# A six-layer windowed-attention stack on one core: the mask goes to VectorE, key norms move into the score banks, and all five instruction orders are rewritten

## The reference

```python
def attn_layer(x, Wqkv, qs, ksc, Wo):                 # 16 heads of 64, windows of 32 tokens
    q, k, v = split(x @ Wqkv)
    q = rotate(l2norm(q) * qs, scale)                 # q*cos + rotate_half(q)*sin
    k = rotate(l2norm(k) * ksc, 1 / scale)
    sim = einsum(q, [previous window of k, own window of k]) * 8.0
    sim = where(mask, -big, sim)                      # a query sees its own 32 keys before it and itself
    return (softmax(sim) @ v) @ Wo
def ffn_layer(x, g, bln, W1, b1, W2, b2):             # 128 -> 2 x 341 -> 128
    xn = (x - mean) / sqrt(var + 1e-5) * g + bln
    a, gate = split(xn @ W1 + b1)
    return a * gelu(gate) @ W2 + b2
for i in range(6):
    x = attn_layer(shift_tokens(x), ...) + x          # half of the features come from the token before
    x = ffn_layer(shift_tokens(x), ...) + x
```

## Time and profile before

| | |
|---|---|
| three runs | 2286.56, 2294.89, 2439.66 us; median 2294.89 us |
| profiled execution | 2313.61 us, span of the instructions 2311.9 us |
| busy, share of the span | PE 89%, DVE 70%, POOL 40%, ACT 39% |
| mean granted TensorE clock | 0.931 of 2.4 GHz |

### The profile page before, as it was taken

How to read it: one execution, slowest core, us unless ns; L and a number is a source line. 1 busy time by engine, 2 the same in 40 slices (tenths; PEclk the granted TensorE clock), 3 DMA queues, 4 the chain that set the end, 5 groups by cost and what they waited for, 6 DMA issues and landing times.

```text
span 2311.9 us, 48227 instructions
## 1 busy us (share of the span) xinstructions
PE 2061.6 (89%) x20232; PEld 920.0 (40%) x20232; DVE 1622.5 (70%) x2739; ACT 911.6 (39%) x1388; POOL 922.6 (40%) x726
## 2 busy tenths in 40 slices
PE   5999948999999999899999999999999998999984
...
DMA packets 104046, 131.55 MB, mean 57 GB/s; under 512 B 28530, under 2 KB 48144, under 8 KB 103824
## 3 DMA queue, kind: packets, MB, share of 16 engines
...
## 4 chain that ended last, share of the span: by engine, by line
PE 52%; DVE 24%; POOL 9%; SPq 5%; ACT 4%; DMA 3%; issue 3%; POOLq 0%; DVEq 0%; ACTq 0%
PE ps_z L1065 11%; PE ps_r L983 8%; SPq L427 4%; DVE t L724 4%; PE ps_s L1041 4%; PE ps_z L1016 4%; PE ps_z L991 4%; POOL prob L500 3%; POOL prob L496 3%; DMA t<-t 3%; PE ps_z L1058 3%; DVE sinv L756 2%; DVE prob L752 2%; DVE t L657 2%; PE ps_r L1093 2%
## 5 line engine op out<-in xcount | busy, mean ns | idle before, releaser
L724 DVE TENSOR_TENSOR t<-ps_r,rot 128x1024 f32<-128x1024 f32 x384 | 461.5, 1211 | 209.6 <-PE ps_r L983 151.2
L983 PE MATMUL ps_r<-xs,w_qk_sb 128*128 128x512 f32 x768 | 430.4, 643 | 96.8 <-ACT sq L552 96.7
L552 ACT ACTIVATE sq<-ps_r 128x512 f32<-128x512 f32 x384 | 229.0, 596 | 499.9 <-DVE t L724 497.1
L490 POOL TENSOR_TENSOR q_hat<-t 128x512 f32<-128x512 f32 x192 | 243.6, 1270 | 322.0 <-DMA t<-t 322.0
L1065 PE MATMUL ps_z<-z,vo 128*128 128x512 f32 x768 | 350.0, 599 | 2.2 <-ACT z L574 2.2
L490 POOL TENSOR_TENSOR k_hat<-t 128x512 f32<-128x512 f32 x192 | 243.6, 1273 | 266.0 <-DMA t<-t 265.8
L496 POOL TENSOR_TENSOR prob<-prob,rnorm 128x1024 f32<-128x1024 f32 x96 | 182.7, 1903 | 375.5 <-DVE prob L752 375.5
L574 ACT ACTIVATE z<-ps_z 128x512 f32<-128x512 f32 x384 | 213.4, 601 | 201.2 <-PE ps_z L1058 200.0
L983 PEld LDWEIGHTS ps_r<-xs,w_qk_sb 128*128 128x128 f32 x768 | 122.5, 192 | 318.4 <-ACT sq L552 217.8
L1041 PEld LDWEIGHTS ps_s<-k_hat,q_hat 64*32 64x32 f32 x12288 | 199.7, 115 | 91.1 <-issue 91.1
L1041 PE MATMUL ps_s<-k_hat,q_hat 64*32 64x64 f32 x12288 | 232.6, 230 | 0.0
...
## 6 DMA issues: line engine op xcount, KB each, us to landing
t<-t SPq DMA_DIRECT2D x1536, 64.0 KB, 2.0
...
z<-q_hat SPq DMA_DIRECT2D x128, 16.0 KB
...
```

Of the source, the lines that this page charges most:

```text
L490: nc.gpsimd.tensor_tensor(dst, t12[:, slot, 0, :], t2[:, slot, :], ALU.add).then_inc(added.sem, 1)
L552: nc.scalar.activation(sq[:, n % SQ_SLOTS, :], ps_r[n % 2][:, :], ACT.Square).then_inc(squared.sem, 1)
L724: nc.vector.tensor_tensor(t12[:, slot, :, :], ps_r[n % 2][:, :].unsqueeze(1).to_broadcast([P, 2, SEQ]), rot[:, n // PAIRS, :, :], ALU.mult ...
L983: nc.tensor.matmul(ps_r[n % 2][:, :], w_qk_sb[:, n, :], xs[:, seq, WIN:WIN + SEQ], start=True, stop=True).then_inc(projected.sem, 1)
```

## The change

1. **Mask.** A score step now fills both banks of a tile, without the mask product: 64 small products, ordered so that even heads (rows 0 to 63, bank 0) and odd heads (rows 64 to 127, bank 1) take turns after every four. There are four score steps a unit instead of eight. DVE **mask** adds the mask while it moves both banks to `prob` (SBUF), **max** reads `prob`, and a new POOL step **lower** subtracts the maximum. `prob` has three slots instead of two. The next score step waits for the mask step of the tile before, where before it waited for the subtraction of two steps earlier.
2. **Norms.** sums 0 and 1, nturn 0, nback and the spreads use the banks `ps_s` instead of `ps_z`. The key factors are split into three bf16 parts (`split_rk`, four more small DVE instructions), so that nback and the eight spread products run in bf16.
3. **Two DMAs a chunk.** Features of a head are stored in pairs (`PAIRED`, on the host), so the swap is between neighbouring partitions: two DMAs of 64 rows with a partition step of 2 instead of four of 32 rows.
4. **Later feed-forward.** It has lag 3 instead of 1 and 2; `xg` is gone (`gain` writes `xc`), x1 waits for `new` of the unit before; `load_ffn` is issued one sequence later.
5. **Order.** All four tables are new.

```diff
 TENSOR_STEPS = [
-    ("rows", 0, 2), ("score", 0, 1), ("nturn", 1, 1), ("hid", 0, 2), ("score", 3, 1), ("hid", 1, 2), ("score", 2, 1),
+    ("out", 0, 2), ("project", 15, 1), ("nback", 0, 1), ("mean", 0, 3), ("xturn", 0, 1), ("spread", 0, 1),
...
-                for r in range(4):
-                    there = r + 1 - 2 * (r % 2)
-                    sync.dma_start(t2[WIN * there:WIN * (there + 1), slot, :],
-                                   t12[WIN * r:WIN * (r + 1), slot, 1, :]).then_inc(swapped[slot].sem, 16)
+                for odd in range(2):
+                    sync.dma_start(t2[1 - odd::2, slot, :], t12[odd::2, slot, 1, :]).then_inc(swapped[slot].sem, 16)
...
+                elif kind == "lower":
+                    pool.wait_ge(top_found.sem, top_found.at(u, n))
+                    s = prob[:, (TT * u + n) % P_SLOTS, :, :, :].rearrange("p c e n -> p (c e) n")
+                    nc.gpsimd.tensor_tensor(s, s, top[:, (TT * u + n) % P_SLOTS, :].unsqueeze(2).to_broadcast([P, HEADS, 2 * WIN]), ALU.subtract).then_inc(lower.sem, 1)
                 elif kind == "scale":
                     pool.wait_ge(normed.sem, normed.at(u, 1))
-                    pool.wait_ge(lowered.sem, lowered.all(u, (2 * n, 2 * n + 1)))
+                    pool.wait_ge(lower.sem, lower.at(u, n))
...
+            def split_rk(u):
+                dve.wait_ge(n_settled.sem, n_settled.done(u))
+                nc.vector.tensor_copy(hi, whole).then_inc(n_split.sem, 1)
+                dve.wait_ge(n_split.sem, n_split.done(u, 0))
+                nc.vector.tensor_tensor(rest, whole, hi, ALU.subtract).then_inc(n_split.sem, 1)
+                dve.wait_ge(n_split.sem, n_split.done(u, 1))
+                nc.vector.tensor_copy(mid, rest).then_inc(n_split.sem, 1)
+                dve.wait_ge(n_split.sem, n_split.done(u, 2))
+                nc.vector.tensor_tensor(low, rest, mid, ALU.subtract).then_inc(normed.sem, 1)
...
-                    nc.vector.tensor_tensor(k, k, ps_z[:, 2:4, :], ALU.mult).then_inc(keyed.sem, 1)
+                    nc.vector.tensor_tensor(k, k, ps_s[:, :, :], ALU.mult).then_inc(keyed.sem, 1)
+                elif kind == "mask":
+                    dve.wait_ge(scored.sem, scored.at(u, n))
+                    nc.vector.tensor_tensor(prob[:, (TT * u + n) % P_SLOTS, :, :, :].rearrange("p c e n -> p e c n"), ps_s[:, :, :].rearrange("p e (c n) -> p e c n", n=2 * WIN),
+                                            band[:, 0 if n == 0 else 1, :].unsqueeze(1).unsqueeze(1).to_broadcast([P, 2, PAIRS, 2 * WIN]), ALU.add).then_inc(masked.sem, 1)
                 elif kind == "max":
...
-                elif kind == "sub":
...
-                        ins = nc.tensor.transpose(ps_z[:, 2, P * t:P * (t + 1)], rk_pad[:, t, :], ident[:, :])
+                        ins = nc.tensor.matmul(ps_s[:, 0, P * t:P * (t + 1)], rk_pad[:, t, :], ident_bf[:, :], start=True, stop=True)
...
-                        ins = nc.tensor.matmul(ps_z[:, 2 + k, :], sel_rows[WIN * j:WIN * (j + 1), n // 2, :], rk_rows[WIN * j:WIN * (j + 1), :],
+                        ins = nc.tensor.matmul(ps_s[:, k, :], sel_rows_bf[WIN * j:WIN * (j + 1), n // 2, :], rk_rows[WIN * j:WIN * (j + 1), :],
...
-                    t, e = n // 2, n % 2
-                    pe.wait_ge(lowered.sem, lowered.at(u, n - 2) if t else lowered.at(u - 1, n - 2 + 2 * TT))
+                    pe.wait_ge(masked.sem, masked.at(u, n - 1) if n else masked.at(u - 1, TT - 1))
...
-                    nc.tensor.matmul(ps_s[:, e, :], ident_bf[:, :], band_bf[:, 0 if t == 0 else 1, :].unsqueeze(1).to_broadcast([P, PAIRS, 2 * WIN]),
-                                     start=True, stop=False, skip_group_check=True)
-                    rows = slice(64 * e, 64 * e + 64)
                     for c in range(PAIRS):
-                        for w in range(4):
...
+                        for e in range(2):
+                            rows = slice(64 * e, 64 * e + 64)
+                            for w in range(4):
```

More of the change, by code:

```diff
@@ L79 @@
-    ("project", 10, 0), ("out", 0, 1), ("nturn", 0, 0), ("project", 11, 0), ("out", 1, 1), ("project", 12, 0),
-    ("nback", 0, 0), ("project", 13, 0), ("spread", 0, 0), ("out", 2, 1), ("project", 14, 0), ("spread", 1, 0),
-    ("project", 15, 0), ("out", 3, 1), ("spread", 2, 0), ("sums", 2, 0), ("mean", 0, 1), ("spread", 3, 0),
-    ("vo", 0, 1), ("var", 0, 1), ("sums", 3, 0), ("score", 1, 0),
+    ("out", 0, 2), ("project", 15, 1), ("nback", 0, 1), ("mean", 0, 3), ("xturn", 0, 1), ("spread", 0, 1),
@@ new lines @@
+    ("sums", 3, 1), ("var", 0, 3), ("out", 1, 2), ("rows", 0, 3), ("spread", 1, 1), ("out", 2, 2), ("spread", 2, 1),
+    ("nturn", 1, 1), ("hid", 0, 3), ("spread", 3, 1), ("out", 3, 2), ("vo", 0, 2), ("hid", 1, 3), ("score", 0, 1),
+    ("hid", 2, 3), ("score", 1, 1), ("project", 0, 0), ("score", 2, 1), ("down", 0, 3), ("project", 1, 0),
+    ("xturn", 1, 1), ("project", 2, 0), ("score", 3, 1), ("project", 3, 0), ("mix", 0, 1), ("project", 4, 0),
+    ("project", 5, 0), ("mix", 1, 1), ("project", 6, 0), ("project", 7, 0), ("sums", 0, 0), ("project", 8, 0),
@@ L83 @@
+    ("project", 9, 0), ("mix", 2, 1), ("project", 10, 0), ("sums", 1, 0), ("project", 11, 0), ("nturn", 0, 0),
+    ("project", 12, 0), ("mix", 3, 1), ("project", 13, 0), ("project", 14, 0), ("sums", 2, 0),
 ]
 VECTOR_STEPS = [
-    ("max", 6, 2), ("sub", 7, 2), ("sub", 6, 2), ("rotate", 2, 1), ("flip", 2, 2), ("rotate", 3, 1), ("psum", 3, 2),
-    ("rotate", 4, 1), ("rotate", 5, 1), ("flip", 3, 2), ("rotate", 6, 1), ("rotate", 7, 1), ("rotate", 8, 1),
-    ("rotate", 9, 1), ("rotate", 10, 1), ("newton", 0, 1), ("rotate", 11, 1), ("rotate", 12, 1), ("rotate", 13, 1),
@@ L88 @@
-    ("keyed", 0, 1), ("rotate", 14, 1), ("keyed", 1, 1), ("rotate", 15, 1), ("x1", 0, 2), ("keyed", 2, 1),
-    ("center", 0, 2), ("keyed", 3, 1), ("rstd", 0, 2), ("max", 1, 1), ("gain", 0, 2), ("sub", 1, 1), ("max", 0, 1),
-    ("newton", 1, 1), ("gated", 0, 2), ("sub", 0, 1), ("max", 3, 1), ("sub", 3, 1), ("gated", 1, 2), ("max", 2, 1),
-    ("sub", 2, 1), ("psum", 0, 1), ("max", 5, 1), ("gated", 2, 2), ("max", 4, 1), ("flip", 0, 1), ("psum", 1, 1),
-    ("sub", 5, 1), ("sub", 4, 1), ("new", 0, 2), ("rotate", 0, 0), ("max", 7, 1), ("flip", 1, 1), ("rotate", 1, 0),
@@ L93 @@
-    ("psum", 2, 1),
+    ("newton", 0, 1), ("rotate", 13, 1), ("rotate", 14, 1), ("rotate", 15, 1), ("center", 0, 3), ("keyed", 0, 1),
+    ("rstd", 0, 3), ("keyed", 1, 1), ("gain", 0, 3), ("keyed", 2, 1), ("keyed", 3, 1), ("gated", 0, 3),
+    ("newton", 1, 1), ("gated", 1, 3), ("mask", 0, 1), ("max", 0, 1), ("gated", 2, 3), ("mask", 1, 1),
+    ("rotate", 0, 0), ("max", 1, 1), ("mask", 2, 1), ("max", 2, 1), ("new", 0, 3), ("psum", 0, 1), ("rotate", 1, 0),
+    ("x1", 0, 2), ("rotate", 2, 0), ("flip", 0, 1), ("psum", 1, 1), ("mask", 3, 1), ("rotate", 3, 0), ("max", 3, 1),
@@ L110 @@
+    ("pnorm", 0, 3), ("scale", 2, 3), ("add", 0, 2), ("add", 1, 2), ("pnorm", 1, 3), ("add", 2, 2), ("lower", 3, 3),
+    ("add", 3, 2), ("scale", 3, 3), ("pnorm", 2, 3), ("add", 4, 2), ("add", 5, 2), ("add", 6, 2), ("pnorm", 3, 3),
+    ("add", 7, 2),
 ]
@@ L436, in swap @@
                     load_vo(layer + 1)
[L437 removed]
+                if seq == 2 and c == 2 and layer:
                     sp.wait_ge(x_new.sem, x_new.done(layer * BATCH - 1))
```

170 lines of the change are left out of this document (84 added, 86 removed).

## The result

The changed kernel takes 2173.65 us (median of four runs, 2169.41 to 2175.08) against 2306.3 us for the kernel before (median of four; one of them, 2439.66 us, is from a slower state of the chip and is left out of the ratio). The ratio of the times is 0.945, 95% interval 0.937 to 0.953: faster by 5.5%. The forecast was 2095 us, range 2015 to 2200. The profiled execution took 2173.78 us, span 2172.1.

The account below looks back on a forecast made before the run. PE bounds the old kernel, DVE next. Stretches of 24.8, 36.3 and 6.8 us plus 0.9 layer work, 1.6 clock dip and 0.6 hand-overs give 71.0 us a unit; with the ends, span 2112, forecast 2095 us, range 2015 to 2200.

Parts of the forecast that it names:

- TensorE's work: PE's work in one unit falls from 71.9 to 62.8 us through mask product (2.4), scores (3.4) and norms (3.3).
- score tile: Score step of 128 instructions for both banks: 1.2 us, near full overlap of the row halves (1.03; without overlap 2.06).
- the rival of the dear DMA: Swap DMAs: an issue of 64 rows costs twice, a chunk takes 2.5 us again; +5 a unit, about 2210 us; chance 0.06.
- Stretch B: From the first score to the last pnorm, POOL's lowers, other passes and adds set the pace while PE waits: 36.3 us.
- C: End of a unit: last flip, PE's wait, last mix, two projections and sums: 6.8 us.
- 10 us of slack: DVE stays at 58 us a unit and keeps 10 us of slack, so masks on DVE leave the time at the forecast.
- stretch A: From the first out to the first score, PE runs without a pause: 24.8 us; DVE has its slack here.
- The ends: Part-filled passes at start and end: first center at 491 us, 86 us for the last passes, last center at 2068.
- the clock dip of 1.6 us: After a pause PE runs 3.5 us at 0.55 of full speed; one such dip a unit, as now, adds 1.6 us.
- the factor 0.992: From profiled execution to median time: the earlier profiled run was 0.8% above its median, so 2114 becomes 2097 us.
- The slower rival: Score tile: taking turns stops the overlap inside a bank, a tile takes 7.4 us, some 2670 us in all; slower: chance 0.04.
- The rival that the mask on VectorE only trades work: Mask step: moving the mask to DVE could simply trade PE work for DVE work; no separate chance given.

Follow-up runs that it names:

- the roots in PSUM: The changed kernel with the scratch of its inverse square roots kept in PSUM's score and sum banks instead of SBUF: 2116.2 us, 0.9195 of the kernel before.

## Why the prediction was right, and where it was off

**TensorE's work.** 62.8 us a unit was forecast, 63.15 came. The mask product is confirmed (0.27 for 0.30), the spreads too (0.32 for 0.3). The score tile was mis-sized, 1.41 for 1.2: of the 1.03 us that full overlap of two steps would save, 0.65 is saved, 0.40 of it by taking turns.

**SyncE and the rival of the dear DMA.** The rival is out: 64 rows cost what 32 do (596 and 590 ns by the medians). Halving the issues is worth 50 us on the old kernel alone and 93 us in the new one. The forecast priced a chunk of 2.5 us at 5 us a unit; 93 us are 3.9 a unit. The runs say that this is the largest single part, that tile overlap and mask product are worth 21 and 26, and that the parts don't add up: each frees a stretch that another engine then paces.

**Stretch B, "the chain is on POOL".** This step failed. Its length was nearly right (from the first score to the next out, B and C, 44.16 us, 1326.03 to 1370.19, for 43.1), but for the wrong engine. GpSimd really runs nearly without gaps in the second part, and that was read as the pace. Without 7.6 us of GpSimd's work nothing moved, with 1.4 us more of TensorE's nothing moved, and without 3.9 us of VectorE's the stretch got 3.7 shorter. VectorE has 38 us of its own work in 39. The 57 to 61 us a unit of VectorE with "10 us of slack" hid this: nearly all of the slack is in stretch A. GpSimd has about 4 us of room in B; held up by more, as with four DMAs, the stretch does grow (41.99 us, 1309.50 to 1351.49 there). It follows that in the first part the waits of TensorE are the other side of VectorE's pace, and moving TensorE's own steps didn't fill them. In the last 15 us three engines are full at once, and which of them is ahead there stays open. That fits a chain that runs 68% over TensorE with the roots in PSUM, while work added to TensorE in the first part lengthens nothing.

**Stretch A.** 24.8 us was forecast, 27.35 came (1370.19 to 1397.54), and 24.78 with the roots in PSUM. The step that failed is "PE runs without a pause": it left newton 0 at its old price. The "four small instructions, 0.24 each" of the split came as forecast (means of 195 to 225 ns), and the 239 ns of the earlier trace rows was the shortest of three sister lines. Another one of the kernel before shows the stall:

```profile
L701 DVE TENSOR_TENSOR n_tmp<-n_tmp,n_half 128x64 f32<-128x64 f32 x144 | 46.6, 323 | 5.0
```

The kernel before has 39 such long instructions, the changed one 97. It is the new order that puts GpSimd's additions beside the roots, and not the quicker transfers: the old order with two DMAs has 26, the new order with four DMAs has 97. VectorE's busy time in the span is 88 us higher with the roots in SBUF (1672.5 against 1584.4). The Trainium skill, page "SBUF — State Buffer", section "SBUF: two separate sides", has the rule: VectorE (with two SBUF inputs against a GpSimd instruction that reads SBUF, or in a mode that uses both its ports) and GpSimd share a pair of ports under an exclusive lock, held for a whole instruction. The trace agrees: 1.30 us for an instruction of 0.22 beside an addition of 1.3, and none above 0.23 once one operand lies in PSUM. Mask and rotate, with one operand in PSUM, stay at 1.16 to 1.23 us, additions or not.

**The ends and the sum.** The first center came at 502.1 for 491, the last at 2128.0 for 2068. With the roots in PSUM they come at 492.6 and 2067.0, and the span is 2110.8 us for the forecast's 2112. So the 60 us by which the span was missed have the size of that one unforeseen cost. That the rest agrees to a microsecond is partly luck. With the roots in PSUM the 21 full steps take 70.4 us on average for 71.0, and the last two together 95.5 us for 86. B and C were a microsecond short, the long steps of each layer (75 against 71 us) cost more than the 0.9 a unit allowed, some 10 us of it through the scaling of `rot`, while the clock dip of 1.6 us that was added to every unit came in fewer than half (12 of the 21 full steps show a granted clock of 1.00). Another 17 us of the miss are the factor 0.992 for the profiled execution, which came out at 1.000: its 0.8% above a median of three scattered runs said nothing. The last 2 are the rounding to 2095.

**The slower rival** (turn-taking that stops the overlap) is refuted: alternating halves are faster than separate ones by 0.40 us a tile. The rule of the Trainium skill, page "TensorE: Matmul & The Clock Gate", section "Wait — 56ns, not 53.3ns?", on 25 ns between starts, which the prediction weighed, doesn't hold for these tiles: 128 in 1.41 us is one every 11 ns.

**The rival that the mask on VectorE only trades work** was put aside with VectorE's slack, and that reason doesn't hold: the masks stand in the very stretch that VectorE paces. VectorE's work a unit stayed the same all the same (60.92 and 60.91 us in the units picked out of the two traces). No run moved the mask step alone.

**What stays open.** The new order, the later feed-forward and the norms in bf16 were not tried alone; the old tables don't fit the new steps. Their share in the gain is what the single parts leave: on the way from the old kernel with two DMAs (2258) to the new one (2174) lie 84 us, of which the tile overlap is 21 and the mask product 26 in the new kernel, and nothing in the old one. So some 40 to 60 us stand behind the rest, and no run divides them.
